# Silu experts' tail: six places for the lines of results, and GpSimd adds the last tile's lines

## The reference, cut to what matters

```
topk_w, topk_idx = top_k(softmax(x2d @ wg_router.T), 6)
topk_w = topk_w / (sum(topk_w) + 1e-20)
...
ye = einsum('ecf,efd->ecd', silu(g) * u, w_down)
y_tok = ye[flat_idx, safe_pos] * vmask
y = sum(y_tok.reshape(T, 6, D) * topk_w[..., None], axis=1)
sh = silu(x2d @ ws_gate) * (x2d @ ws_up) @ ws_down
x = x + y + sh
```

## Time and profile before

| | us |
|---|---|
| median of 3 runs | 1113.92 |
| lowest and highest | 1109.98 and 1114.08 |
| the profiled execution | 1115.0 |
| its span | 1113.2 |

### The profile page before, as it was taken

One profiled execution on the slowest core, in us unless ns is written; L12 is line 12 of the kernel. 1 busy time (PEld: TensorE's weight loads), 2 busy tenths in 40 slices (PEclk: granted clock), 3 DMA queues, 4 the chain that ended last, 5 costly groups with the idle time before them and its releaser, 6 DMA issues. The chain is left out here.

```text
span 1113.2 us, 16699 instructions
## 1 busy us (share of the span) xinstructions
PE 1033.7 (93%) x6084; PEld 869.2 (78%) x6084; DVE 756.4 (68%) x1346; ACT 595.3 (53%) x1055; POOL 564.1 (51%) x412
## 2 busy tenths in 40 slices
PE   5899999999999999999998989998978887999991
PEld 4788888888888888888887776664766687999991
DVE  4777764777657776667774545466788755888877
ACT  3566664666545666456662433342433245888871
POOL 1575633756236564355540246773334777655552
PEclk9899999999999999999999899999998998999996
DMA  7210220001600992000000226661301346677666
GB/s 202 51 34 1 44 52 1 20 5 39 57 1 7 239 226 59 1 1 1 1 1 6 74 101 211 211 199 57 109 1 52 133 168 231 224 239 234 231 217 204
DMA packets 45343, 109.79 MB, mean 99 GB/s; under 512 B 8487, under 2 KB 25525, under 8 KB 43216
## 3 DMA queue, kind: packets, MB, share of 16 engines
q1 hardware_dynamic: 38352, 95.46, 30.1%
q0 software_dynamic: 6912, 13.30, 3.2%
HBM read 94.27 MB, written 41.29 MB: 122 GB/s over the span
## 5 line engine op out<-in xcount | busy, mean ns | idle before, releaser
L460 POOL TENSOR_TENSOR at_prob<-at_prob,at_inv_sum 128x1024 f32<-128x1024 f32 x128 | 243.8, 1907 | 273.7 <-DVE at_inv_sum L678 273.7
L641 ACT ACTIVATE at_pt_h<-ps 128x512 fp32r<-128x512 f32 x256 | 139.3, 596 | 139.9 <-PE ps L566 139.8
L729 DVE TENSOR_TENSOR at_pt_l<-ps,at_pt_h 128x512 fp32r<-128x512 f32 x256 | 164.6, 685 | 60.9 <-ACT at_pt_h L641 60.9
L718 DVE TENSOR_REDUCE at_neg_max<-ps 128x1 f32<-128x1024 f32 x128 | 154.7, 1209 | 36.9 <-PE ps L41 36.5
L608 ACT ACTIVATE at_prob<-ps,at_neg_max 128x1024 f32<-128x1024 f32 x128 | 143.7, 1123 | 15.1 <-DVE at_neg_max L718 15.1
L566 PE MATMUL ps<-ident,at_prob 128*128 128x128 f32 x1024 | 133.8, 274 | 5.1 <-POOL at_prob L460 3.9
L566 PEld LDWEIGHTS ps<-ident,at_prob 128*128 128x128 f32 x1024 | 119.3, 140 | 23.0 <-POOL at_prob L460 4.7
L2128 POOL DMA_INDIRECT lines<-f_y,f_x_raw x96 | 97.4, 1015 | 71.5 <-ACT f_y L2045 42.1
L39 PE MATMUL ps<-at_k_h,at_q_h 128*128 128x512 f32 x256 | 108.4, 423 | 0.0
L39 PE MATMUL ps<-at_pt_h,at_v_h 128*128 128x512 f32 x256 | 100.3, 392 | 0.0
L40 PE MATMUL ps<-at_k_l,at_q_h 128*128 128x512 f32 x256 | 100.2, 391 | 0.0
(11 more groups left out here) (319 smaller groups left out, 2459.5 us busy)
## 6 DMA issues: line engine op xcount, KB each, us to landing
e_raw<-in_we SPq DMA_DIRECT2D x32, 624.0 KB, 4.3
f_cw_row<-cw SPq DMA_DIRECT2D x32, 512.0 KB, 4.2
slots<-in_empty SPq DMA_DIRECT2D x4, 3456.0 KB, 41.2
f_x_raw<-slots SPq DMA_DIRECT2D x32, 432.0 KB, 4.9
lines<-in_empty SPq DMA_DIRECT2D x3, 2048.0 KB, 33.2
f_e_raw<-in_we SPq DMA_DIRECT2D x32, 128.0 KB, 2.6
at_wq_raw<-in_wq SPq DMA_DIRECT2D x4, 512.0 KB, 4.0
at_wo_raw<-in_wo SPq DMA_DIRECT2D x4, 512.0 KB, 3.5
```

The costliest lines, as they stand in the source:

```text
L460: nc.gpsimd.tensor_tensor(prob[:, t % RING, :], prob[:, t % RING, :], inv_sum[:, t:t + 1].broadcast_to([P, T]), ALU.mult).then_inc(normed, 1)
L641: nc.scalar.activation(pt_h[:, e[1] % PT, :], turned(e[1]), ACT.Copy).then_inc(pt_high, 1)
L718: nc.vector.tensor_reduce(neg_max[:, t:t + 1], slot(n, start), AX.XY, ALU.max, negate=True).then_inc(maxed, 1)
L729: nc.vector.tensor_tensor(pt_l[:, e[1] % PT, :], turned(e[1]), pt_h[:, e[1] % PT, :].bitcast(F32), ALU.subtract).then_inc(pt_split, 1)
```

## The change

There are six places in place of three: `row`, `xn_h`, `xn_l` as before for m = 0, 1, 2, and for m = 3, 4, 5 the buffers `net.shared1_h`, `net.shared1_l` and `net.raw`, whose weights have been used up by then (8 KB for each partition, without gaps). Three semaphores signal the landings in turn. The waits of the loads for VectorE's additions are gone. From the fourth load on, each waits instead until the load three before it has landed; the second half of the last region waits for the landing of m = 3.

Of the eight tiles VectorE adds the first seven. The lines of the eighth (LAST = 7) are added by GpSimd behind its last scatter: for each m a product of lines and share into a new buffer `weighed_line`, then x plus this buffer, each a 128 x 256 instruction that waits for the one before it. The store of tiles 6 and 7 also waits for these twelve instructions (`tile_added`). In the attention, far ahead, two semaphores (`ready`, `bo_added`) become one (`prepared`) that counts both events.

```
-        PLACES = len(lines)
+        lines += [ap[:, 0:TT * D].bitcast(F32).rearrange("p (i d) -> p i d", d=D) for ap in (net.shared1_h, net.shared1_l)]
+        lines += [net.raw[:, 0:TT * D].rearrange("p (i d) -> p i d", d=D)]
+        SIGNALS = 3
+        LAST = TT - 1
+        weighed_line = sb("weighed_line", [P, D])
...
         def lines_added(m, i):
-            return TT // 2 + TT * m + i
+            return TT // 2 + LAST * m + i
+        def line_signal(m, h=0):
+            return lines_loaded[(m + h) % SIGNALS], 16 * ((m + h) // SIGNALS + 1)
...
-                    if m >= PLACES:
-                        sp.wait_ge(y_added, lines_added(m - PLACES + 1, 0))
+                    if m >= SIGNALS:
+                        sp.wait_ge(*line_signal(m - SIGNALS))
...
                     if h:
-                        sp.wait_ge(y_added, lines_added(TOP1 - PLACES + 1, 0))
-                    sp.dma_start(lines[last_place(h)][:, half, :], part[:, half, :]).then_inc(lines_loaded[last_place(h)], 16)
+                        sp.wait_ge(*line_signal(TOP1 - 1 - SIGNALS, 1))
+                    sp.dma_start(lines[TOP1 - 1][:, half, :], part[:, half, :]).then_inc(line_signal(TOP1 - 1, h)[0], 16)
                 for k in range(TT // 2):
-                    sp.wait_ge(y_added, lines_added(TOP1 - 1, 2 * (k + 1)))
+                    sp.wait_ge(y_added, lines_added(TOP1 - 1, min(2 * (k + 1), LAST)))
+                    if k == TT // 2 - 1:
+                        sp.wait_ge(tile_added, 2 * TOP1)
...
                 for n in range(EXP1):
                     combine(n)
+                pool.wait_ge(routed, places(NB - 1) + 1)
+                pool.wait_ge(seeded, TT // 2)
+                for m in range(TOP1):
+                    j = TOP1 - 1 - m
+                    pool.wait_ge(*line_signal(m, 1 if m == TOP1 - 1 else 0))
+                    nc.gpsimd.tensor_tensor(weighed_line[:, :], lines[m][:, LAST, :], share[:, LAST, j:j + 1].broadcast_to([P, D]),
+                                            ALU.mult).then_inc(tile_added, 1)
+                    pool.wait_ge(tile_added, 2 * m + 1)
+                    nc.gpsimd.tensor_tensor(net.x[:, LAST, :], net.x[:, LAST, :], weighed_line[:, :], ALU.add).then_inc(tile_added, 1)
+                    pool.wait_ge(tile_added, 2 * m + 2)
...
-                add_lines(0, range(2, TT))
+                add_lines(0, range(2, LAST))
                 for m in range(1, TOP1):
-                    add_lines(m, range(TT))
+                    add_lines(m, range(LAST))
```

More of the change, by code:

```diff
@@ L311, in softmax_attention_phase @@
         norm = Norm(nc, net, "n0", mem, load=True, xc=prob[:, RING - 2:, :].rearrange("p r (k d) -> p (r k) d", d=D))
-        consts, ready = sem("consts"), sem("ready")
+        consts, prepared = sem("consts"), sem("prepared")
         wq_loaded, wk_loaded, wv_loaded, wo_loaded = sem("wq_loaded"), sem("wk_loaded"), sem("wv_loaded"), sem("wo_loaded")
@@ L316, in softmax_attention_phase @@
         bq_scaled = sem("bq_scaled")
-        bo_added = sem("bo_added")
+        ONE, BIASED = 1, 2
         proj_full, proj_read = sem("proj_full"), sem("proj_read")
@@ L481, in group @@
                             nc.gpsimd.tensor_tensor(net.x[:, :, :], net.x[:, :, :],
-                                                    bo[:, :].unsqueeze(1).broadcast_to([P, TT, D]), ALU.add).then_inc(bo_added, 1)
-                nc.gpsimd.memset(one[:, :], 1.0).then_inc(ready, 1)
-                pool.wait_ge(ready, 1)
+                                                    bo[:, :].unsqueeze(1).broadcast_to([P, TT, D]), ALU.add).then_inc(prepared, 1)
+                nc.gpsimd.memset(one[:, :], 1.0).then_inc(prepared, 1)
+                pool.wait_ge(prepared, ONE)
                 norm.wait(pool, "xc_done", TT)
@@ L740, in run @@
                             if g == KV - 1:
-                                dve.wait_ge(bo_added, 1)
+                                dve.wait_ge(prepared, BIASED)
                             add_to_x(nc, net, e[1] * TT // 2, slot(n, start)).then_inc(y_added, 1)
@@ L1760, in silu_experts_phase @@
         lines = [row[:, :, 0:D]] + [ap[:, :, :].bitcast(F32).rearrange("p c (i d) -> p (c i) d", d=D) for ap in (xn_h, xn_l)]
-        PLACES = len(lines)
+        lines += [ap[:, 0:TT * D].bitcast(F32).rearrange("p (i d) -> p i d", d=D) for ap in (net.shared1_h, net.shared1_l)]
[3 more added lines that the diff above has]
+        weighed_line = sb("weighed_line", [P, D])
         consts = sem("consts")
-        y_added, x_stored = sem("y_added"), sem("x_stored")
+        y_added, x_stored, tile_added = sem("y_added"), sem("x_stored"), sem("tile_added")
         scores, routed, ranked = sem("scores"), sem("routed"), sem("ranked")
@@ L1775, in silu_experts_phase @@
         y_weighed, combined = sem("y_weighed"), [sem("combined0"), sem("combined1")]
-        lines_loaded, seeded = [sem(f"lines_loaded{m}") for m in range(PLACES)], sem("seeded")
+        lines_loaded, seeded = [sem(f"lines_loaded{m}") for m in range(SIGNALS)], sem("seeded")
         def blocks(ap):
@@ L1832, in lines_added @@
         def lines_added(m, i):
-            return TT // 2 + TT * m + i
-        def last_place(h):
-            return (TOP1 - 1 + h) % PLACES
+            return TT // 2 + LAST * m + i
+        def line_signal(m, h=0):
+            return lines_loaded[(m + h) % SIGNALS], 16 * ((m + h) // SIGNALS + 1)
         def turned_bank():
@@ L1886, in _ @@
                     sp.wait_ge(*adds(EXP1 - 1 - j))
-                    if m >= PLACES:
-                        sp.wait_ge(y_added, lines_added(m - PLACES + 1, 0))
+                    if m >= SIGNALS:
+                        sp.wait_ge(*line_signal(m - SIGNALS))
                     part = net.lines[j * T:(j + 1) * T, :].rearrange("(p i) d -> p i d", p=P)
                     if m < TOP1 - 1:
-                        sp.dma_start(lines[m % PLACES], part).then_inc(lines_loaded[m % PLACES], 16)
+                        sp.dma_start(lines[m], part).then_inc(line_signal(m)[0], 16)
                 for h in range(2):
@@ L2247, in add_lines @@
                     for i in tiles:
-                        place = last_place(i // (TT // 2)) if m == TOP1 - 1 else m % PLACES
                         acc = ps[:, ACC_BANKS[i // 2], (i % 2) * D:(i % 2 + 1) * D]
                         if i == tiles[0] or m == TOP1 - 1 and i == TT // 2:
-                            dve.wait_ge(lines_loaded[place], 16 * (m // PLACES + 1 if place == m % PLACES else (m + 1) // PLACES + 1))
+                            dve.wait_ge(*line_signal(m, i // (TT // 2) if m == TOP1 - 1 else 0))
                         if m == 0:
@@ L2256, in add_lines @@
                         to = net.x[:, i, :] if m == TOP1 - 1 else acc
-                        nc.vector.scalar_tensor_tensor(to, lines[place][:, i, :], share[:, i, j:j + 1], acc,
+                        nc.vector.scalar_tensor_tensor(to, lines[m][:, i, :], share[:, i, j:j + 1], acc,
                                                        ALU.mult, ALU.add).then_inc(y_added, 1)
```

## The result

The changed kernel is slower: 1117.36 us median of 16 runs (1112.79 to 1119.65), against 1111.21 us of 16 runs of the kernel before beside them (1107.8 to 1114.08). The ratio is 1.0049, 95% interval 1.0036 to 1.0062, that is 4.0 to 6.9 us. The profiled execution took 1119.65 us, its span 1117.9.

What follows compares the result with a forecast made beforehand. Bound by the landing of m = 4 behind step 30's third scatter, sixteen VectorE additions and a store; 0.79 + 1.06 = 1.85 us saved, 1113.92 to 1112.1 us; own range 1111.5 to 1113.1, with run spread 1108.2 to 1115.0.

Steps and rivals of the forecast that it cites:

- GpSimd's twelve instructions: Tail, behind GpSimd's last scatter: six pairs of 1.5 us end at 1107.4, 1.4 us before VectorE, so cost is hidden.
- The rival on the slower side: From m = 4's landing on, VectorE and GpSimd block each other at SBUF: 2.7 us lost, 0.85 slower, 1114.8; chance 0.10.
- Two additions fewer behind the landing of m = 4: VectorE's end of the tail: 14 additions in place of 16 behind that landing, 0.79 us saved on the path.
- The place of m = 3: Load into a gapless buffer lands sooner, step 30's third scatter lands at 1097.6, m = 4 at 1103.2: 1.06 us gained.
- the rival by which the scatter gains nothing: Step 30's third scatter: m = 4 lands at 1104.26 as before, only 0.79 us saved, 1113.1; chance 0.25.
- The last store: End of the tail, behind the last additions: 2.2 us to landing, 2.6 with issue and closing, taken as unchanged.
- GpSimd's pairs: Product plus addition on GpSimd behind its last scatter: 0.614 and 0.739 us, with waits 1.5 us a pair.
- Taking the waits from m = 3 and m = 4: SP's loads in the tail: gives nothing by itself, since a scatter ended both waits.
- The merged semaphore: In the attention: changes neither an order nor an instruction's length, so nothing either way.

Runs made afterwards that it cites:

- without GpSimd: Changed kernel without GpSimd's part: six places and loads as changed, VectorE adds all eight tiles; ratio to the kernel before 1.0002 (0.9977 to 1.0027).
- the two later profiles before: The unchanged kernel before, profiled twice more; from the start of TensorE's closing drain to the end 22.2 and 21.9 us, first profile 24.0.
- drain at step 24: Changed kernel with one more GpSimd drain, ahead of the scatters of step 24; ratio to the kernel before 0.9999 (0.9977 to 1.0022).
- six drains: Changed kernel with six more GpSimd drains, ahead of the scatters of steps 4, 8, 12, 16, 20 and 24; ratio to the kernel before 1.0029.
- drain at step 16: Changed kernel with one more GpSimd drain, ahead of the scatters of step 16; ratio to the kernel before 1.0012 (0.9991 to 1.0033).
- fewer scatters: Changed kernel sending only the first of three scatters for experts up to step 25, 92 indirect transfers, not 144; ratio to the kernel before 1.0039.

## Why the prediction was wrong

The forecast was 1112.1 us, 1.85 less than before. The step that failed is the one on GpSimd's twelve instructions: "nothing of GpSimd's queue stands behind", and so its cost "is hidden behind VectorE" with 1.4 us to spare, since "Nothing waits for GpSimd but the last store". The instructions were hidden: the last ended 0.06, 1.4 and 1.0 us before VectorE's last addition in the three profiles after. But behind them stood the drain that closes GpSimd's queue, 9.2 us long with 144 indirect transfers, and the end of the program waited for it. The cover that counted was not the one up to VectorE's last addition. Before the change the drain ended 6.7 us ahead of SP's (1106.3 against 1113.0); the change moved GpSimd's last instruction back by 11.15 us (1097.08 to 1108.23), while TensorE's closing drain began 0.9 us later. I had priced the instructions and the waits between them, not what follows an engine's last instruction. The row was in the trace: a drain of 12.6 us under the block's line. I had read only the busy rows and SP's.

The rival on the slower side, engines taking turns at a way into SBUF, was not it. VectorE's additions stayed 0.393 us apart beside GpSimd's ((2.84 - 0.48) / 6; without GpSimd (3.23 - 0.48) / 7, the same), and GpSimd's additions took 0.72 us, with 0.74 forecast. The Trainium skill states in "SBUF — State Buffer", section "Who interferes with whom", that a VectorE instruction with at most one SBUF input does not contend with GpSimd. In "DVE: scalar operands, raw-bit mode, write accounting and state across instructions", section "Scalar operands", it states that a pointer scalar does not take up the second tensor stream. The 0.393 us agree with both: the column of shares did not count as a second SBUF input here.

The other terms, against the profiles:

- Two additions fewer behind the landing of m = 4, 0.79 us: right. Fourteen took 5.62 us (1102.67 to 1108.29), sixteen 6.35.
- The place of m = 3, 1.06 us: its landing and the scatter were right in kind and sized from one slow execution. m = 3 landed 4.9, 4.9 and 5.5 us after its issue in three profiles after; before it took 7.4 in the first, but 5.7 and 5.6 in the two later. The third scatter of step 30 took 4.69, 4.76 and 4.96 us after, 6.02, 5.48 and 5.09 before. The load of m = 4 took 4.84 to 5.05 us after and 4.63 and 4.69 in the two later profiles before; the 5.93 on which I built part of the gain was one execution's. Counted from the start of TensorE's closing drain, VectorE began with m = 4 after 12.7, 13.0 and 13.1 us, before after 15.1, 13.3 and 13.0: by the medians 0.3 us are gained, not 1.06, which is nearer to the rival by which the scatter gains nothing.
- The last store, taken as unchanged: it landed 2.5 us after its issue in place of 2.2, and SP's drain came 2.8 us behind VectorE's last addition in place of 2.4, in three profiles each. So SP's end came 0.3 to 0.9 us earlier than in the two later profiles before, in place of 1.85.
- GpSimd's pairs: 1.5 us each, right. The last ended 18.2 us behind the start of TensorE's closing drain (1108.23 - 1090.0), 17.2 and 17.6 in the later profiles, forecast 18.3 (1107.4 - 1089.1). That this is so close is partly luck: the second half of m = 5 went out sooner than forecast (9.5 us behind that start, not 11.2) and took 7.2, 6.1 and 6.6 us to land, not 5.9. By its own 1100.3 and 5.9 us the forecast should have had it land at 1106.2, not 1105.9.
- Taking the waits from m = 3 and m = 4: not tried by itself; in the profile after SP waited for scatters ahead of both, as before. The merged semaphore: nothing to be seen, the attention ends at 609.1 before and 609.2 after.

So the gain in the tail was smaller than its sum, and the end was set by something that wasn't in the sum.

## What to carry to other kernels

Before giving an idle engine the last piece of work, look at what closes its queue: find the drains under the line of the block, add each one's length behind its engine's last instruction, and compare with the engine that ends last. Here GpSimd, with 144 indirect transfers since its last drain, had one of 9.2 us, and work put behind its last scatter moved the drain by as much. A difference of two profiles is no better than the spread of one kernel's profiles: the tail of the kernel before alone varied by 2.1 us.

## What the runs showed of the hardware

The closing drain of GpSimd grows with the indirect transfers that it has sent since its last drain, and not with the time since they landed: the additions behind the last scatter, 11 us of them, didn't shorten it.

| indirect transfers since the drain before | drain, us | for each |
|---|---|---|
| 24 (drain at step 24, six drains) | 2.02, 2.01 | 0.084 |
| 48 (drain at step 16) | 3.98 | 0.083 |
| 92 (fewer scatters) | 7.58 | 0.082 |
| 144 (three profiles of the changed kernel) | 9.21 | 0.064 |

Up to 92 it is 0.083 us for each. At 144 it is as long as for 111 (9.21 / 0.083), and the drain midway with 120 ended 8.9 us behind its scatters, not 10; that some of them are cleared earlier would explain it, but was not tried. The time since the drain before doesn't fit in place of the count: 3.98 us came after 90 us, 7.58 us after 260. And the table is for drains well behind the last scatter: the five of 12 transfers midway, right behind their scatters, ended 3.7 to 5.1 us after them, not 1.0.

The linear attention is longer where TensorE's granted clock is lower. Its mean over that phase is 0.98 in the profiles in which the phase takes 84.9 us and 0.96 in those in which it takes 86.4 to 86.6, whichever the kernel. One stretch, first in the profile before, then in the one after (stretch, its length, busy time of PE, PEld, DVE, ACT, POOL, granted clock, DMA share, GB/s):

```profile
794.00:798.00 4.00, 3.92 (x57) 3.32 (x58) 1.79 (x3) 2.05 (x6) 1.92 (x2) 1.00 0.97 330
```

```profile
794.00:798.00 4.00, 4.00 (x16) 3.52 (x16) 0.91 (x2) 0.63 (x2) 0.00 (x0) 0.51 1.00 348
```

At 0.51, the 1.2 GHz level, TensorE was busy throughout and got less done: the same twelve products (L39 to L41, ahead of L1361) took 2.22 us in the profile before (792.88 to 795.10) and 4.01 in the one after (793.12 to 797.13). From 786 to 790 us, still at 1.00 in both, TensorE was busy for 3.92 of the 4 us in either. The 1.6 us between 84.9 and 86.5 us are part of the 6.3 us over which the 16 runs of the kernel before spread; the rest was not looked into.
